# Projections of a graph attention layer: three tiles by fifteen products in place of two tiles by seven

## The reference

```python
Q, K, V = ((x @ W).reshape(N, 8, 64) for W in (Wq, Wk, Wv))
score = exp(clip(einsum('ehd,ehd->eh', K[src], Q[dst]) / 8, -5, 5))[..., None]
h = x + segment_sum(V[src] * score, dst) / (segment_sum(score, dst) + 1e-6)
y = x + (h - mean(h, 0)) * rsqrt(var(h, 0) + 1e-5) * gamma + beta   # over the nodes
out = (y - y.mean(1)) / sqrt(y.var(1) + 1e-5)                       # over the features
```

## Time and profile before

| | us |
|---|---|
| median of 3 runs | 1910.76 (1909.86 to 1912.99) |
| the profiled execution | 1908.01 |
| its span, first to last instruction | 1906.1 |
| TensorE busy | 1861.6 (98%) |
| VectorE busy | 1697.0 (89%) |
| ScalarE busy | 1367.5 (72%) |
| POOL busy | 1291.3 (68%) |
| mean granted TensorE clock | 0.994 |

### The profile page before, as it was taken

How to read it: one execution, slowest core, us unless ns; L and a number is a source line. 1 busy time by engine, 2 the same in 40 slices (tenths; PEclk the granted TensorE clock), 3 DMA queues, 4 the chain that set the end, 5 groups by cost and what they waited for, 6 DMA issues and landing times.

```text
span 1906.1 us, 41424 instructions
## 1 busy us (share of the span) xinstructions
PE 1861.6 (98%) x7904; PEld 1362.2 (71%) x8014; DVE 1697.0 (89%) x2454; ACT 1367.5 (72%) x4602; POOL 1291.3 (68%) x1473
## 2 busy tenths in 40 slices
PE   7999999998999999999999999999999999999897
PEld 4555555554888888878888888888888888887333
DVE  6677755644999999999999999999999999999888
ACT  0002000002999999999999999999999999998857
POOL 0205666103777888788888888888888888885677
PEclk9999999999999999999999999999999999999999
DMA  5547788546999999999999999999999999999307
GB/s 183 162 151 250 288 319 274 186 161 231 357 358 356 362 367 358 346 351 368 368 356 353 352 366 369 354 355 355 366 361 358 360 355 365 370 358 370 122 33 287
DMA packets 184521, 589.09 MB, mean 309 GB/s; under 512 B 28480, under 2 KB 30240, under 8 KB 184480
## 3 DMA queue, kind: packets, MB, share of 16 engines
q0 software_dynamic: 135904, 465.14, 65.8%
q1 hardware_dynamic: 45120, 121.69, 17.8%
q10 hardware_dynamic: 3456, 1.78, 0.3%
HBM read 535.27 MB, written 78.91 MB: 322 GB/s over the span
## 4 chain that ended last, share of the span: by engine, by line
PE 74%; DVE 16%; issue 4%; DMA 4%; ACT 1%; POOL 1%; SPq 0%; DVEq 0%; ACTq 0%; POOLq 0%
PE acc L939 29%; PE places L342 22%; PE q_ps L923 17%; DVE kv L795 6%; DVE raw L806 5%; DMA kv<-kv_d,idx 2%; PE mm_ps L949 2%; PE banks L1151 1%; DVE stats L1288 1%; DVE agg L1281 1%; PE mm_ps L951 1%; PE places L402 1%; DMA q_tile<-xb_d 1%; POOL kv L751 1%; PE banks L1142 1%
## 5 line engine op out<-in xcount | busy, mean ns | idle before, releaser
L751 POOL DMA_INDIRECT kv<-kv_d,idx x880 | 887.0, 1008 | 339.2 <-issue 204.8
L846 ACT ACTIVATE kv<-kv 128x64 f32<-128x64 f32 x3520 | 889.0, 335 | 14.3
L939 PE MATMUL acc<-kv,mm_sb 128*128 128x260 f32 x3520 | 845.6, 383 | 4.1 <-POOL kv L714 2.2
L939 PEld LDWEIGHTS acc<-kv,mm_sb 128*128 128x128 f32 x3520 | 654.3, 190 | 137.9 <-issue 32.8
L923 PE MATMUL q_ps<-q_tile,mm_sb 128*128 x1760 | 559.2, 439 | 5.6 <-DVE kv L795 4.9
L795 DVE TENSOR_TENSOR kv<-q_ps,kv 128x1024 f32<-128x1024 f32 x440 | 536.1, 1218 | 14.0 <-PE q_ps L923 7.0
L806 DVE TENSOR_REDUCE raw<-kv 128x16 f32<-128x1024 f32 x440 | 532.2, 1210 | 0.0
L923 PEld LDWEIGHTS q_ps<-q_tile,mm_sb 128*128 128x128 f32 x1760 | 328.6, 189 | 74.4 <-DVE kv L795 20.8
L714 DVE TENSOR_TENSOR kv<-kv 128x384 f32<-128x384 f32 (+1 forms) x440 | 271.6, 617 | 0.1
L857 ACT ACTIVATE mm_sb<-mm_ps,less 128x1024 fp32r<-128x1024 f32 x220 | 241.2, 1096 | 13.1 <-remote 10.1
L435 ACT COPY p<-places 128x768 f32<-128x768 f32 x23 | 18.4, 798 | 243.5 <-PE places L342 243.5
(11 more groups left out here) (171 smaller groups left out, 1358.6 us busy)
## 6 DMA issues: line engine op xcount, KB each, us to landing
q_tile<-q_d SPq DMA_DIRECT2D x49, 512.0 KB, 7.2
kv<-kv_d,idx POOLq DMA_INDIRECT x880, 6.2
kv_d<-kv_a SPq DMA_DIRECT2D x25, 512.0 KB, 5.5
xb<-in_x POOLq DMA_DIRECT2D x49, 256.0 KB, 4.3
xb_d<-xb POOLq DMA_DIRECT2D x49, 256.0 KB, 3.7
out_rows<-agg SPq DMA_DIRECT2D x49, 256.0 KB, 2.1
x_sb<-in_xT SPq DMA_DIRECT2D x24, 512.0 KB, 7.9
q_d<-q_a SPq DMA_DIRECT2D x24, 512.0 KB, 4.1
```

The source lines that it names most:

```text
L751: pool.indirect_dma_start(kv[:, s, u, 0:2 * DIM], None, kv_d, bass.IndirectOffsetOnAxis(idx[:, s, u:u + 1], 0), bounds_check=N_NODES - 1, ...
L846: return act.activation(v, v, ACT.Copy, scale=kv[:, s, u, 2 * DIM + h:2 * DIM + h + 1])
L939: last = pe.matmul(acc[:, bass.ds(par, 1), DIM - (1 - n) * HALF:DIM + n * HALF], m, kv[:, sc, u, DIM + n * HALF:DIM + (n + 1) * HALF], sta ...
```

## The change

Sixteen "trios" of three tiles take the place of the duos. A trio is a 3 x 2 by 2 x 3 product of blocks: three tiles, two halves of the inputs, three matrices (Wq, Wk, Wv as the blocks, 512 columns each). It is done by fifteen products in place of eighteen, each of 2 chunks x 512 columns. The odd 49th tile is computed plainly, and first: K, Q, V. The new names: `B00` to `B12` are weight blocks (half of inputs, matrix: 0 is K, 1 is Q, 2 is V), `T0` to `T14` sums of weight blocks (eleven, made once), `X0` to `X13` sums of x blocks (eleven per trio, in four groups `x_sums_first` to `x_sums_last`), and `M1` to `M13`, `T`, `U` hold partial results in SBUF. PSUM has eight places of one bank. Six products accumulate on top of an earlier one, once ScalarE or VectorE has read that one. x has two slots of three tiles in place of three slots of two. All numbers of the result go through VectorE's 14 instructions of decoding (`s_dec`) and ScalarE's 6 copies (`s_kc`) per trio. K and V are stored as blocks of 128 x 512. The transposes stand at trio 8, behind the last decoding of trio 7. TensorE's list of one trio:

In the fence above the waits are given as comments in short form. The diff of the rest, cut to its core:

```diff
+                if g == 1:
+                    sp.wait_ge(s_prod, 3)
+                elif g > 1:
+                    sp.wait_ge(s_prod, made(g - 2, 15))
+                sp.dma_start(x_sb[:, g % 2, :, :, :],
+                             xT[3 * g:3 * g + 3].rearrange("t p c n -> p t c n")).then_inc(s_x[g % 2], 16)
...
+            for g in range(TRIOS):
+                if 0 < g < TRIOS - 1:
+                    load(g + 1)
...
+                sp.wait_ge(s_kc, copied(g, 4))
+                store_k(c, k_out(2), s_kva)
+                sp.wait_ge(s_dec, decoded(g, 3))
+                store_v(b, v_out(1), s_kvb)
+                store_q(a, split_of(g, 0), q_a, s_qa)
+                sp.wait_ge(s_dec, decoded(g, 7))
+                store_k(a, k_out(0), s_kva)
+                sp.wait_ge(s_dec, decoded(g, 8))
+                store_k(b, k_out(1), s_kva)
+                sp.wait_ge(s_dec, decoded(g, 11))
+                store_v(a, v_out(0), s_kvb)
+                sp.wait_ge(s_dec, decoded(g, 12))
+                store_v(c, v_out(2), s_kvb)
+                store_q(b, split_of(g, 1), q_b, s_qb)
+                store_q(c, split_of(g, 2), q_c, s_qc)
...
+                if g == TABLE_TRIO:
                     pe.wait_ge(s_visit, 3)
+                    pe.wait_ge(s_dec, decoded(g - 1, 14))
...
+                act.wait_ge(s_prod, made(g, 1))
+                wait(act, s_dec, decoded(g - 1, 8))
+                act.copy(held(M5), place(BANK_5)).then_inc(s_kc, 1)
+                act.wait_ge(s_prod, made(g, 2))
+                wait(act, s_dec, decoded(g - 1, 14))
+                act.copy(held(M9), place(BANK_9)).then_inc(s_kc, 1)
+                act.wait_ge(s_prod, made(g, 3))
+                wait(act, s_dec, decoded(g - 1, 12))
+                act.copy(held(M2), place(BANK_2)).then_inc(s_kc, 1)
+                act.wait_ge(s_prod, made(g, 4))
+                act.wait_ge(s_kva, 16 * (1 + 3 * g))
+                act.copy(k_out(2), place(BANK_5)).then_inc(s_kc, 1)
                 for b in digits_after(3 * g):
                     sign(b)
+                act.wait_ge(s_prod, made(g, 7))
+                if g:
+                    act.wait_ge(s_split, 2 * split_of(g - 1, 1))
+                act.copy(held(M13), place(BANK_13)).then_inc(s_kc, 1)
+                act.wait_ge(s_prod, made(g, 11))
+                wait(act, s_dec, decoded(g - 1, 11))
+                act.copy(held(M1), place(BANK_1)).then_inc(s_kc, 1)
...
+            for g in range(TRIOS):
+                if g == TABLE_TRIO:
                     dve.wait_ge(s_tr, 1)
+                    dve.tensor_copy(src_t[:, :], places[:, 0:2, :].rearrange("p a n -> p (a n)")[:, 0:VCOLS]).then_inc(s_trc, 1)
+                dve.wait_ge(s_prod, made(g, 5))
+                dve.wait_ge(s_kc, copied(g, 1))
+                dve.wait_ge(s_split, 2 * (split_of(g, 0) - 1))
+                dve.tensor_tensor(held(T), place(BANK_9), held(M5), ALU.subtract).then_inc(s_dec, 1)
+                dve.wait_ge(s_prod, made(g, 6))
+                dve.tensor_tensor(held(U), place(BANK_2), held(M5), ALU.add).then_inc(s_dec, 1)
                 tables(3 * g)
+                dve.wait_ge(s_prod, made(g, 7))
+                dve.wait_ge(s_kvb, 16 * (1 + 3 * g))
+                dve.wait_ge(s_dec, decoded(g, 2))
+                dve.wait_ge(s_kc, copied(g, 5))
+                dve.tensor_tensor(v_out(1), place(BANK_13), held(U), ALU.subtract).then_inc(s_dec, 1)
+                dve.tensor_tensor(held(M13), held(M13), held(M9), ALU.add).then_inc(s_dec, 1)
+                dve.wait_ge(s_prod, made(g, 8))
+                dve.tensor_tensor(held(T), held(T), place(BANK_0), ALU.subtract).then_inc(s_dec, 1)
+                dve.wait_ge(s_dec, decoded(g, 5))
+                dve.tensor_tensor(held(M9), held(M9), held(T), ALU.subtract).then_inc(s_dec, 1)
+                split(q_a, held(T), split_of(g, 0), s_qa, 16 * g)
+                if g + 1 < TRIOS:
+                    x_sums_first(g + 1)
+                dve.wait_ge(s_prod, made(g, 9))
+                dve.wait_ge(s_kc, copied(g, 4))
+                dve.tensor_tensor(k_out(0), place(BANK_9), held(M5), ALU.subtract).then_inc(s_dec, 1)
+                dve.wait_ge(s_prod, made(g, 10))
+                dve.scalar_tensor_tensor(out=k_out(1), in0=place(BANK_2), scalar=-1.0, in1=held(M5),
+                                         op0=ALU.mult, op1=ALU.subtract).then_inc(s_dec, 1)
                 tables(3 * g + 1)
+                if g + 1 < TRIOS:
+                    x_sums_second(g + 1)
+                dve.wait_ge(s_kc, copied(g, 6))
+                dve.tensor_tensor(held(M1), held(M1), held(M2), ALU.add).then_inc(s_dec, 1)
+                dve.tensor_tensor(held(M2), held(M2), v_out(1), ALU.add).then_inc(s_dec, 1)
+                dve.wait_ge(s_prod, made(g, 12))
+                dve.wait_ge(s_dec, decoded(g, 9))
+                dve.tensor_tensor(v_out(0), place(BANK_0), held(M1), ALU.add).then_inc(s_dec, 1)
+                dve.wait_ge(s_prod, made(g, 13))
+                dve.wait_ge(s_dec, decoded(g, 10))
+                dve.tensor_tensor(v_out(2), place(BANK_3), held(M2), ALU.subtract).then_inc(s_dec, 1)
                 tables(3 * g + 2)
+                dve.wait_ge(s_prod, made(g, 14))
+                dve.tensor_tensor(held(M13), place(BANK_1), held(M13), ALU.subtract).then_inc(s_dec, 1)
+                dve.wait_ge(s_dec, decoded(g, 13))
+                split(q_b, held(M13), split_of(g, 1), s_qb, 16 * g)
+                if g + 1 < TRIOS:
+                    x_sums_third(g + 1)
+                dve.wait_ge(s_prod, made(g, 15))
+                dve.wait_ge(s_split, 2 * split_of(g, 0))
+                dve.tensor_tensor(held(T), place(BANK_7), held(M9), ALU.add).then_inc(s_dec, 1)
+                dve.wait_ge(s_dec, decoded(g, 14))
+                split(q_c, held(T), split_of(g, 2), s_qc, 16 * (g + 1))
+                if g + 1 < TRIOS:
+                    x_sums_last(g + 1)
...
-            pe.wait_ge(soft["s_kc"], TILES // 2 + 3)
+            pe.wait_ge(soft["s_kc"], 2 + 6 * (TILES // 3))
+            pe.wait_ge(soft["s_dec"], 14 * (TILES // 3) - 6)
```

More of the change, by code:

```diff
@@ L338, in _, with product @@
         def _(pe):
-            def product(out, left, right, fresh=True, told=True):
+            def product(bank, left, right, fresh):
                 for c in range(DEEP):
-                    for cols in (slice(0, DIM), slice(DIM, SIDE)):
-                        last = pe.matmul(out[:, cols], left[:, c, :], right[:, c, cols], start=fresh and c == 0,
-                                         stop=c == DEEP - 1, skip_group_check=True)
-                if told:
-                    last.then_inc(s_prod, 1)
@@ L347, in by_sum @@
-            def by_sum(g, n, k):
-                pe.wait_ge(s_sums, 4 * g + k)
-                wait(pe, s_wt, k if g == 0 else 0)
-                product(place(g, n), s_sb[:, g % 2, k - 1, :, :], t_sb[:, k - 1, :, :])
-            pe.wait_ge(s_x[X_DUOS - 1], 16)
-            lone = x_sb[:, X_DUOS - 1, 0, :, :]
-            pe.wait_ge(s_wk, 16 * CHUNKS)
-            for c in range(CHUNKS):
-                pe.matmul(place(-1, 5)[:, 0:DIM], lone[:, c, :], w_sb[:, c, DIM:2 * DIM], start=c == 0,
-                          stop=c == CHUNKS - 1)
@@ L359, in _, with lone @@
-            pe.wait_ge(s_wq[0], 16)
-            for g in range(LAST):
-                if g == TABLE_DUO:
+                    last = pe.matmul(place(bank), left[:, c, :], right[:, c, :], start=fresh and c == 0,
+                                     stop=c == DEEP - 1, skip_group_check=True)
+                last.then_inc(s_prod, 1)
+            def lone(bank, j):
+                for c in range(CHUNKS):
+                    last = pe.matmul(place(bank), x_sb[:, 1, 0, c, :], w_sb[:, 3 * (c // DEEP) + j, c % DEEP, :],
+                                     start=c == 0, stop=c == CHUNKS - 1)
+                last.then_inc(s_prod, 1)
@@ L371, in _ @@
-                if g == 0:
-                    pe.wait_ge(s_wv, 16)
-                    for c in range(CHUNKS):
-                        last = pe.matmul(place(-1, 5)[:, DIM:2 * DIM], lone[:, c, :],
-                                         w_sb[:, c, 2 * DIM:3 * DIM], start=c == 0, stop=c == CHUNKS - 1)
-                    last.then_inc(s_prod, 2)
-                wait(pe, s_c22, g)
-                if g == TABLE_DUO:
-                    pe.wait_ge(s_trc, 1)
-                by_sum(g, 1, 2)
@@ L399, in plain @@
-            def plain(out, left, n):
-                for c in range(CHUNKS):
-                    last = pe.matmul(out, left[:, c, :], w_sb[:, c, n * DIM:(n + 1) * DIM], start=c == 0,
-                                     stop=c == CHUNKS - 1)
-                return last
-            a, b = (x_sb[:, LAST % X_DUOS, n, :, :] for n in range(2))
-            pe.wait_ge(s_x[LAST % X_DUOS], duo_x(LAST))
-            pe.wait_ge(s_u, 3 * (LAST - 1) + 2)
-            plain(place(LAST, 0)[:, 0:DIM], a, 1)
```

381 lines of the change are left out of this document (189 added, 192 removed).

## The result

The changed kernel is slower: 1921.5 us (median of 9 runs, 1915.5 to 1928.1) against 1910.8 us (9 runs, 1906.2 to 1913.4), ratio 1.0062 (1.0048 to 1.0075). The forecast was 1902.8 us, with a range of 1894 to 1914; the sign is that of rival 3, 5 us beyond its 1916.4. The profiled execution took 1916.45 us, 8.4 more than the one of before; it is the second shortest of its nine.

The account below looks back on a forecast made before the run. TensorE's products were taken to bound the projections. Columns -24.0, handover +7.0, fewer Q stores -1.0, barrier +6.0, POOL's additions and x loads +4.0 gave -8.0 us: 1900.0 in the profile's terms, 1902.8 us as median, range 1894 to 1914.

Parts of the forecast that it names:

- rival 3: Projections: port and VectorE decide, 2.4 us over the slack per trio, 17.6 in all; +5.6, 1916.4 us; chance 0.11.
- term 1: TensorE's projections: fewer columns save 24.0 us (bounds 23.2 and 24.3), ending at 435.2 us if it never waits.
- term 2: Handover to the gathers: first gather 0.4 us after TensorE's end instead of 6.6 before it, giving back 7.0 us.
- The −1.0 for fewer stores of Q: Behind the first gather: one Q store falls there instead of three, -1 us (-2.5 to 0).
- 5.9 of slack: VectorE's dense row per trio: 3.8 us behind product 14 plus 2.1 us of waiting inside the row absorb delays.
- term 3: Barrier at trio 8: TensorE waits for trio 7's last T before the transposes, 6 us (2.4 to 8).
- terms 3 and 4: Projections: 6.0 us for the barrier at trio 8, 4.0 us for POOL's additions and x loads over seven trios.
- the prediction's walk: VectorE's instruction order through a trio, timed from its first product; trio 7's last T comes 6.3 us after product 15.
- Rival 2: Projections: x's two slots set a 27.0 us loop per trio over 25.75; -2, 1908.8 us; chance 0.18.
- rival 4: Handover: POOL's moved chain ends behind the projections, needing to be 29 us late; 1911 us or more; chance 0.03.
- Rival 1: Projections: the slack holds everything, leaving only 2.4 us at the barrier; -15.6, 1895.2 us; chance 0.25.
- The waits in quiet trios: TensorE gaps before 200 us, which would show the forecast wrong altogether; no stall was expected there.

Follow-up runs that it names:

- e6: e5 with the transposes behind product 4 of trio 8 instead of ahead of product 1; ratio 0.9919 to the kernel before.
- e11: The changed kernel itself, run again on the chip of e9 and e10; ratio 1.006 to the kernel before.
- e1: Changed kernel with POOL adding beta in one column of 512 only, all transfers kept; ratio 0.9932 to the kernel before.
- e3: Changed kernel with digits, and ScalarE's signs with them, moved out of VectorE's dense row from trio 7 on; ratio 0.9987 to the kernel before.
- e5: Changed kernel with all 49 full additions paced, three or four a trio from trio 1, each group released by its trio's second product; ratio 0.993 to the kernel before.
- e9: e7 with every table piece, signs and POOL's table transfers one trio later; ratio 0.9895, 1890.4 us against 1910.3 for the kernel before.
- e2: Changed kernel with the transposes at trio 6 instead of trio 8; ratio 1.0054 to the kernel before.
- e4: Changed kernel with the edits of e2 and e3 together; ratio 0.9967 to the kernel before.
- e10: Changed kernel with beta added in the first 256 of 512 columns only, additions not paced; ratio 0.9954 to the kernel before.
- e7: e6 with the lone tile's Q product moved last and three weight sums behind the first two decodings; ratio 0.9949 to the kernel before.

## Why the prediction was wrong

**Columns (term 1): right.** Trio 0 starts at 22.59 (the terms give 22.5). 110 products on, at 211.4 by 1.716 us each, the first decoding of trio 7 starts at 211.62, so up to there TensorE loses nothing; and e6, in which it never waits, ends at 435.24 (435.2 in the terms).

**Handover (term 2): right.** The first gather starts 0.3 us after TensorE's end (0.4 forecast). The −1.0 for fewer stores of Q behind it did not come: behind the first gather the span is 0.2 us longer than before, and in e11, the same kernel, 3 us longer.

**The step that failed: the size of the excess in VectorE's dense row** ("3.7 to 5.6 us of excess against 5.9 of slack", and in term 3 "about 3.5" for trio 7), in terms 3 and 4 alike. Here is what trio 7's row looked like on VectorE after, and POOL's additions beside it:

```profile
219.76 2.47 DVE L565 SCALAR_TENSOR_TENSOR q_a<-c_sb,q_a 128x512 fp32r<-128x512 f32 x1
...
222.82 1.84 DVE L535 TENSOR_TENSOR s_sb<-s_sb,x_sb 128x256 f32<-128x256 f32 x1
...
226.12 1.63 DVE L575 TENSOR_SCALAR kv<-kv 128x1024 int32<-128x1024 int32 x1
...
228.94 2.17 DVE L696 TENSOR_TENSOR c_sb<-c_sb,kv 128x512 f32<-128x512 f32 x1
...
234.49 1.79 DVE L563 TENSOR_SCALAR q_b<-c_sb 128x512 fp32r<-128x512 f32 x1
...
237.26 1.96 DVE L550 TENSOR_TENSOR s_sb<-x_sb,s_sb 128x256 f32<-128x256 f32 x1
...
239.81 0.68 DVE L712 TENSOR_TENSOR c_sb<-places,c_sb 128x512 f32<-128x512 f32 x1
```

```profile
220.38 1.28 POOL L347 TENSOR_TENSOR xb<-xb,bet 128x512 f32<-128x512 f32 x1
...
223.08 1.29 POOL L347 TENSOR_TENSOR xb<-xb,bet 128x512 f32<-128x512 f32 x1
```

There is one addition about every 2.8 us (the first is at 217.20, more follow up to 237.65), and each met an instruction that could be stretched. Against e1's means for the same groups, VectorE's work from 211 to 240 us is stretched by 9.7 us, 1.9 of that on digits; the last T ends at 240.5, 11.9 us behind product 15, where the prediction's walk had 6.3. Two things were mis-sized. First, the rate of 0.5 to 0.7 us of excess for each us of such work was a mean over the kernel before, where VectorE often works on PSUM or waits while an addition runs: its 23 us are 37% of the 63 us of additions. In the row of trio 7, which has no gap, each of the eight additions before 240 lands: 9.7 us of stretching for their 10.6 us. 7.8 us of that fall on the 7.9 us of work that the prediction had priced at 3.7 to 5.6, a rate of 1.0. Second, the other 1.9 us fall on two digits (681 ns alone, 1.63 us each here), which the prediction had taken at their mean in the kernel before, 788 ns. The prediction speaks of instructions that read two operands from SBUF, but that is not the line: a digit reads one, and so does the first half of a split (0.42 to 1.79 us), which its 23 us (with 3.1) and its 7.9 us hold all the same. Work with an operand in PSUM is not held up, as predicted (0.68 us at 239.81). By groups from 211 to 420 us the stretching is 42.3 us, 67% of all additions.

The additions come in bursts, and the waits follow them. The dense rows of trios 7 to 12, from V of tile b to the last T, meet 8, 8, 6, 4, 2 and 6 additions and are stretched by 9.8, 10.8, 6.6, 3.8, 0.8 and 6.2 us. TensorE waits behind the first three, for long behind the first two, which also hold two digits each; the 6.2 us of trio 12 cost it no wait. That fits the 5.9 us of slack that the prediction had.

The Trainium skill, page "SBUF — State Buffer", section "Who interferes with whom", speaks of a port pair of SBUF that VectorE and GpSimd share, and says that whichever of them has it holds it for a whole instruction and blocks the other. The trace agrees in so far as one meeting can cost more than the addition's length (222.82: 1.84 where 0.41 is such a sum undisturbed, 1.43 more). The prediction had the full 1.28 us for each meeting and then priced by the mean.

**Stalls by place**, from starts, against e6's 435.24 (after ends at 460.60): barrier 12.0 + 0.8 for the transposes + 0.8 for the product behind = 13.6, where 6 stood. Trio 9: 2.86 ahead of product 4, 3.88 ahead of product 5 (0.92 of it the slow product 4), 2.98 in products 5 to 8 = 9.7. Trio 10: 1.5. Small ones and the start 0.5. Together 25.3 us, where terms 3 and 4 had 10. Of this 5.5 us (0.8 + 0.8 + 0.9 + 3.0) are matmuls at a lower granted clock, which the prediction had nowhere: of the 15.3 us that were missed, a third. These 15.3 us and the 1.0 of the stores turn the forecast of −8.0 into the +8.4 of the profiles, to 0.1. The median is 2.3 us beyond that, since it lies 5.1 us above the profiled execution and not 2.8 as before.

**Ahead of product 4** the prediction had expected no wait. ScalarE after, in trio 9:

```profile
275.06 1.15 ACT L465 ACTIVATE kv<-kv,minus 128x1024 bf16<-128x1024 int32 x1 [5.04 <-DVE kv L575]
276.12 0.57 ACT L474 COPY c_sb<-places 128x512 f32<-128x512 f32 x1
```

A sign stands ahead of the copy of M5 and waits for a digit that was itself stretched (it ends at 275.03). So ScalarE's copy inherits VectorE's delay through work that nobody is in a hurry for. In e3, which moves both, no wait for M5 is left; what the sign alone cost was not run.

**The rivals.** Rival 3 had mechanism and sign: its 6 + 17.6 us for terms 3 and 4 stand against 25.3. That they come so near is in part luck: it has 2.4 us in each of seven trios, and what came lies behind three rows, a fifth of it in slow matmuls. It was given 0.11 because "PSUM work and waits lie between", which holds for the mean of the kernel before and not for the row. Rival 2 is out: VectorE waited once for x (3.7 us, the first load), and the 16 loads took 6.6 us at the median. So is rival 4: POOL waited 71 us for the last store. Rival 1 came true once the additions were paced: e5 has the barrier's 2.3 us alone. The waits in quiet trios that would have made all of it wrong did not appear.

## What to carry to other kernels

Price a shared resource in the window that has no slack, not by its mean: there each competing instruction cost about its full length, and what went over the slack was paid by the bound engine, with slower matmuls behind the longer waits on top. When work is moved onto an engine that has average room (here 15.5 of 25.75 us), ask what else runs then; here the same reordering costs 0.6% with free-running additions and gains 0.7% (e5) with fewer of them at a time, let go about where VectorE is idle next; with the transposes later it gains 0.8% (e6), and with a cover for the handover 1.1% (e9). A barrier that shows the longest wait may be where a backlog ends, so look at what is late ahead of it before moving it.

## What the runs showed of the hardware

- An addition on POOL holds up VectorE's single-operand SBUF instructions as well: 128x1024 int32 0.68 us alone, 1.21 on average while additions run, 1.63 when hit. The loss is nearly all on VectorE's side: 47 of POOL's 49 additions keep their 1.27 to 1.30 us in the profile after, two take 1.37 and 1.64.
- A hit can cost VectorE more than the addition lasts: the split at 219.76 took 2.47 us instead of 0.69 (1.78 more) for one addition of 1.28. The rows show a rule for the size: in the profile after, all 36 instructions that were held up end 0.29 to 0.31 us behind the end of the addition (sums of 256 columns, first halves of splits) or 0.55 to 0.57 us behind it (two operands of 512 columns, digits), though they began anywhere from 0.64 us ahead of the addition's start to 1.14 us behind it. So what begins just ahead of an addition loses most: the split began 0.62 us ahead (220.38), and the addition ends at 221.66, the split at 222.23. The mechanism behind it was not looked into, and starts on POOL are rough.
- Waits of 2.7 and 2.96 us of TensorE, 2.6 us of matmul between them, were followed by a granted clock of 0.63 over 7 us and four products in 9.85 us instead of 6.87; the wait of 1.22 us was followed by four products in 6.97. In e5 the transposes behind the wait of 2.29 us take 0.79 us, at a granted clock of 1.00.
- The changed kernel's runs scatter more: 12.6 us between the lowest and the highest of 9, against 7.2 before. So do those of e2, e3, e4 and e11 (8.2 to 12.6), with full additions that run free; where the additions are paced or narrow (e1, e5, e6, e9, e10) it is 1.7 to 3.6, and 5.7 in e7. The meetings of two free-running queues are one possible cause; this was not tested.
